# 1444-key attention on one core: score maxima dealt anew over the key tiles, high keys copied a tile sooner

## The reference

```
qm = _split_heads(q @ Wq.T + bq)      # q: layer-normed x, 32 x 100 x 128
km = _split_heads(k @ Wk.T + bk)      # k = v = ctx_1024, 32 x 1444 x 128
vm = _split_heads(v @ Wv.T + bv)
scores = jnp.einsum('bnlh,bnph->bnlp', qm, km) / sqrt(HEAD_DIM)
attn = jax.nn.softmax(jnp.where(mask, scores, MASK_FILL), axis=-1)
out = jnp.einsum('bnlp,bnph->bnlh', attn, vm)
```

## Time and profile before

| | before |
|---|---|
| median of 3 runs | 2171.78 us (2168.76 to 2175.56) |
| the profiled execution, its own time | 2172.06 us |
| its span in the profile | 2170.3 us |
| PE busy | 1935.4 us (89%) |
| DVE busy | 1481.8 us (68%) |
| ACT busy | 1321.2 us (61%) |
| POOL busy | 670.7 us (31%) |
| first `weigh` of the first batch to the last score product | about 603 to 1670 us of the span |

### The profile page before, as it was taken

One profiled execution on the slowest core, in us unless ns is written; L12 is line 12 of the kernel. 1 busy time (PEld: TensorE's weight loads), 2 busy tenths in 40 slices (PEclk: granted clock), 3 DMA queues, 4 the chain that ended last, 5 costly groups with the idle time before them and its releaser, 6 DMA issues. The chain is left out here.

```text
span 2170.3 us, 42902 instructions
## 1 busy us (share of the span) xinstructions
PE 1935.4 (89%) x16792; PEld 1224.2 (56%) x16792; DVE 1481.8 (68%) x3509; ACT 1321.2 (61%) x2169; POOL 670.7 (31%) x605
## 2 busy tenths in 40 slices
PE   3669999766899999999999999999998899999997
PEld 2536766444465656656566565665655455555553
DVE  4844666785778787777877778777783456577541
ACT  2635677586166666666666666666776345666643
POOL 1410223321422131322313223131221323566576
PEclk9879999877599999999999999999999557999998
DMA  5025555001232332323323232232332102221222
GB/s 157 1 69 189 168 186 172 26 27 47 89 106 82 114 119 72 131 82 114 108 84 131 81 115 97 95 131 68 124 105 75 24 12 45 48 41 36 36 70 42
DMA packets 126293, 190.74 MB, mean 88 GB/s; under 512 B 42018, under 2 KB 99466, under 8 KB 125710
## 3 DMA queue, kind: packets, MB, share of 16 engines
q1 hardware_dynamic: 126094, 188.01, 27.9%
HBM read 104.84 MB, written 11.76 MB: 54 GB/s over the span
## 5 line engine op out<-in xcount | busy, mean ns | idle before, releaser
L1607 DVE TENSOR_REDUCE b_part_max<-psum 128x1 f32<-128x482 f32 (+3 forms) x1248 | 738.6, 650 | 200.8 <-PE psum L1493 186.0
L1413 ACT ACTIVATE b_PT<-psum 128x800 f32<-128x800 f32 x768 | 614.9, 836 | 335.4 <-PE psum L1512 329.5
L1493 PE MATMUL psum<-b_KH,b_QBD 64*128 64x482 f32 (+1 forms) x1152 | 416.2, 441 | 37.4 <-DVE b_part_max L1607 35.0
L1512 PE MATMUL psum<-b_QS,b_KS 64*128 64x200 f32 x3072 | 436.7, 288 | 0.3 <-ACT b_PT L1413 0.3
L1512 PEld LDWEIGHTS psum<-b_QS,b_KS 64*128 64x128 f32 x3072 | 346.2, 187 | 15.2 <-issue 10.5
L1528 PE MATMUL psum<-b_PT,b_V 128*32 128x200 f32 x6144 | 341.4, 339 | 0.3 <-ACT b_PT L1413 0.3
L1493 PEld LDWEIGHTS psum<-b_KH,b_QBD 64*128 64x128 f32 x1152 | 194.1, 189 | 182.1 <-DVE b_part_max L1607 115.7
L1338 POOL TENSOR_TENSOR b_KL<-b_KF,b_KH 128x1444 fp32r<-128x1444 f32 x32 | 106.9, 3340 | 589.7 <-PE psum L1512 566.5
L1528 PEld LDWEIGHTS psum<-b_PT,b_V 128*32 128x32 f32 x6144 | 159.9, 109 | 144.6 <-ACT b_PT L1413 78.7
L1814 POOL TENSOR_TENSOR c_HE<-c_HE,c_G 128x400 f32<-128x400 f32 x128 | 131.5, 1032 | 112.6 <-ACT c_HE L1960 106.0
L426 POOL TENSOR_TENSOR a_rs<-a_ve,a_half 100x4 f32<-100x4 f32 x48 | 48.5, 1011 | 312.6 <-DVE a_ve L918 312.5
(11 more groups left out here) (280 smaller groups left out, 2988.2 us busy)
## 6 DMA issues: line engine op xcount, KB each, us to landing
b_KS<-b_KH SPq DMA_DIRECT2D x64, 722.0 KB
a_CT<-in_ctxt SPq DMA_DIRECT2D x32, 722.0 KB, 5.6
b_CT<-in_ctxt SPq DMA_DIRECT2D x32, 722.0 KB, 4.3
b_KS<-b_KL SPq DMA_DIRECT2D x32, 722.0 KB
a_CN<-in_ctxn SPq DMA_DIRECT2D x32, 704.0 KB
c_G<-gates_scratch SPq DMA_DIRECT2D x16, 800.0 KB, 4.3
att_scratch<-b_AO SPq DMA_DIRECT2D x32, 200.0 KB, 5.8
b_MB<-in_mask SPq DMA_DIRECT2D x32, 180.5 KB, 4.4
```

What stands on the lines that cost most here:

```text
L1413: nc.scalar.activation(PT[:, kt % 2, 2 * a:2 * a + 2, :], psum[:, 2 * a:2 * a + 2, 0:TG], ACT.Exp).then_inc(sem["pt_ready"], 1)
L1493: m = mm(bank(b, D, size), QBD[rows, j % 2, tile * D:(tile + 1) * D], KH[rows, j % 2, at_:at_ + size], start=True, stop=True)
L1512: m = mm(bank(p, D, 2 * T, (s % 2) * 2 * T), KS[rows, j % 2, s, kt * D:(kt + 1) * D], QS[rows, j % 2, s * 2 * T:(s + 1) * 2 * T], start=Tr ...
L1607: v.tensor_reduce(part_max[0:rows, q, c:c + 1], bank(b, rows, CHUNKS[c][1]), AX.X, ALU.max)\
```

## The change

Maxima by key tile, in the order of the batch (upper and lower ones added):

| tile | 8 | 9 | 10 | 11 | 0 | 1 | 2 to 6 | 7 |
|---|---|---|---|---|---|---|---|---|
| before | 0 | 4 | 4 | 4 | 4 | 3 | 3 each | 2 |
| after | 2 | 4 | 3 | 3 | 3 | 4 | 3 each | 2 |

`EARLY`, now the count of those in tiles 8 to 11, stays 12. Because tile 8 now has the first maxima of the batch after next, ahead of the "turn" job of the next one, `part_max` gets two buffers; and ACT copies key chunk c behind the exponentials of tile c + 7 instead of c + 8.

```
-MAIN_TILES = ((9, 2, 2), (10, 2, 2), (11, 2, 2), (0, 2, 2), (1, 2, 1), (2, 1, 2), (3, 2, 1), (4, 1, 2), (5, 2, 1), (6, 1, 2), (7, 1, 1))
+MAIN_TILES = ((8, 1, 1), (9, 2, 2), (10, 2, 1), (11, 1, 2), (0, 2, 1), (1, 2, 2), (2, 1, 2), (3, 2, 1), (4, 1, 2), (5, 2, 1), (6, 1, 2),
+              (7, 1, 1))
...
-EARLY = sum(kt > 8 for _, _, _, kt, _ in MAINS)
+EARLY = sum(kt > 7 for _, _, _, kt, _ in MAINS)
...
-        part_max = sb("part_max", [D, QCH, 3])
+        part_max = sb("part_max", [D, 2, QCH, 3])
...
-            pl.memset(part_max[:, :, :], 0.0)
+            pl.memset(part_max[:, :, :, :], 0.0)
...
-                        if kt - 8 in range(len(keys)):
-                            high_keys(place(g, j, keys[kt - 8]), g, j + 2, kt - 8)
+                        if kt - 7 in range(len(keys)):
+                            high_keys(place(g, j, keys[kt - 7]), g, j + 2, kt - 7)
...
-                    v.tensor_reduce(part_max[0:rows, q, c:c + 1], bank(b, rows, CHUNKS[c][1]), AX.X, ALU.max)\
+                    v.tensor_reduce(part_max[0:rows, n % 2, q, c:c + 1], bank(b, rows, CHUNKS[c][1]), AX.X, ALU.max)\
                         .then_inc(drained, 1)
                     if i == MAXES - 1:
                         dve.wait_ge(drained, done)
-                        v.tensor_reduce(mx[:, 0:QCH], part_max[:, :, :], AX.X, ALU.max, negate=True).then_inc(sem["mx_ready"], 1)
+                        v.tensor_reduce(mx[:, 0:QCH], part_max[:, n % 2, :, :], AX.X, ALU.max, negate=True).then_inc(sem["mx_ready"], 1)
```

## The result

The changed kernel takes 2146.81 us (median of 4 runs, 2140.1 to 2149.43), the kernel before, beside it, 2172.74 (4 runs, 2168.76 to 2175.56): a ratio of 0.9875 [0.9849, 0.9901]. I had forecast 2157.2, in a range from 2147 to 2171. The direction was right; the gain, 26 us, is nearly twice the 14.6 of my sum.

What follows compares the result with a forecast made beforehand. VectorE's reductions were taken to pace the four-maxima tiles, the exponentials' floor of 1.89 us the three-maxima tiles. Tile terms summed to -0.485 us a batch, -14.6 over 30 batches, giving 2157.2 us, range 2147 to 2171.

Steps and rivals of the forecast that it cites:

- Tile 8, +0.59: In tile 8, two maxima more: the key waits for the first maximum's bank; 3.05 us for 2.46, +0.59.
- Tiles 9, 10, 11, 0 and 1: Tile 9: 0; 10, 11, 0: -0.55, -0.56, -0.57 us (-0.47 with three queries); tile 1: +0.55 to +0.59.
- High keys a tile sooner, 0: ScalarE's copies of key chunks, ahead of the next tile's exponentials, are hidden by the wait for scores: cost 0.
- The turn later, 0: VectorE starts the turn 0.8 us later, so the maxima's four DMAs issue later, but land in time: cost 0.
- The sum, -14.6: Tile terms of the attention stage: four batches -1.94 us, a batch -0.485, 30 batches -14.6.
- The floor of 1.89: In the last batch, with no jobs, tiles take 1.86 and 1.92 us in turn: the exponentials set a floor of 1.89.
- VectorE's waits for products: A sign to look for: VectorE's waits for products, 186.0 us, should shrink by about what the span does.
- Rival (a): The ring of banks holds three-maxima tiles at 2.06 us, not 1.90: -0.06 a batch, 2170 us; chance 0.17.
- Rival (b): VectorE alone is the bound and tile 8 fills its hole: 1.0 us a batch, 30 us, 2142; chance 0.12.
- Rival (c): The maxima's DMAs land too late, the first score piece waits: +0.28 us a batch, 2180 us; chance 0.09.
- The step that failed: Whole program: -14.6 us against the profiled execution's 2172.06 gives 2157.5; that execution is 0.3 above the median, so 2157.2.

Runs made afterwards that it cites:

- 13 copies: The kernel before with 13 ScalarE copies, one behind the other, as a pause between the attention stage and the last stage: 2169.35 us, 1.0000 [0.9976, 1.0023].
- 7 copies: The changed kernel with 7 ScalarE copies as a pause between the attention stage and the last stage: 2154.38 us, 0.9918 [0.9890, 0.9946] to the kernel before.
- 8 copies: The changed kernel with 8 ScalarE copies as a pause between the attention stage and the last stage: 2149.40 us, 0.9915 [0.9888, 0.9941] to the kernel before.

## Why the prediction was right in its steps and wrong in its size

- **Tile 8, +0.59.** Right: 3.05, by the mechanism named, the key held by the first reduction.
- **Tiles 9, 10, 11, 0 and 1.** Right within 0.02 us, with the one exception of tile 0 with three queries, 3.62 for 3.71: its queries load at 1005.42, 1005.99 and 1006.55, each released by a reduction, 2.06, 2.63 and 3.19 us into the tile. I had put the third at 3.28; the three reductions came 0.57 apart here and not 0.61. That is 0.09 us in 8 batches, 0.7 us in all.
- **High keys a tile sooner, 0.** Right: alone it is worth nothing in either kernel.
- **The turn later, 0.** Right for the reason given: the last of the four DMAs was issued at 998.81, and the first score product that needs them loads its weights at 1002.26 with no DMA among its releasers. When it landed no row shows.
- **The sum, -14.6.** Measured -14.0 in the stage.
- **The floor of 1.89**, put down to the exponentials: the number held (1.88 to 1.92), the reason is not shown. In the earlier trace rows ScalarE is busy for 1.50 of 1.86 and 1.63 of 1.92, TensorE for all of both; each waits for the other in turn.
- **VectorE's waits for products**, to shrink: they grew by 12.7 us, for the reason given above.
- **Rival (a)**, three-maxima tiles at 2.06: refuted, 1.91 and 1.92. **Rival (b)**, VectorE alone: refuted, VectorE still waits 198.7 us for products and the stage gained 14 us, not 30; that the total came near its 2142 is a coincidence. **Rival (c)**: refuted, no wait for a DMA.
- **The step that failed** stands in no sentence of the forecast, only in its arithmetic: "against the profiled execution's 2172.06 that is 2157.5". It holds that everything outside the stage keeps its time, a term of nothing for which no row was read. The last stage did not: 484.8 us for 497.8, with the granted clock at 0.89 for 0.85. I had read a granted clock of 1.00 in every window of the attention stage and not read the windows behind it, where it is at most 0.59 for 129 us. The 0.3 us by which the profiled execution stood above the median of 3 runs said nothing of a program whose runs spread over 26 us; 66 runs have a median 3 us lower.

The 26 us are made up so: 14 from the dealing, shown tile by tile; about 10, an estimate, from less time at the lower clock, which a pause ahead of the last stage can give without the change (13 copies in the kernel before, shown) and perhaps take back (7 copies, indicated only); about 3 of chance in the runs compared. Why the changed kernel spent less time at the lower clock stays open.

## What to carry to other kernels

A stretch with a known pattern can be priced to some hundredths of a microsecond from stretches that already show the pattern: count jobs against banks, and find the drain that each job waits for. A pattern that no stretch shows yet cannot (2.97 us expected, 3.16 measured, for the value between the halves). But where a program passes through a phase of lower clock, its total time is not the old one less the saving: read the granted clock of every stage beside the edited one, give the range its spread, and judge a change of under one per cent by its own stage, or at equal time at the lower clock. To put a job sooner into a ring of banks is worth nothing while its drainer comes as late as before: here it cost 47 us. With the drainer sooner too, the loss was gone, but nothing was gained.

## What was not expected of the hardware

- A pause that puts off the last stage by 9.5 us cost nothing in the kernel before (1.0000 [0.9976, 1.0023]), while the low time fell by 28 us (333 to 305 on the same chip). In the changed kernel 7 copies, which put it off by 4.1 us, go with 11 us more in the mean (2145.8 to 2157.2), and 8 copies with 5 (2150.9); these runs are not all of one chip.
- A microsecond more at the lower level goes with 0.31 us more of the program's time, not with the 0.5 of a program that TensorE alone bounds. The windows above fit that in kind: in the 30 us from 59 us behind the end of the attention stage, TensorE got through 191 instructions at 0.54 and through 229 at 0.89, only 1.2 times as many, for there it was idle for 7.4 us of the 30 and VectorE busy for 21.27.
- Products of 128 rows put between the two halves' work made that work longer: 1.27 us in two parts, and a tile of 3.17 us with PE busy for all of it, where moving the value was expected to save (2.97). The Trainium skill, "TensorEngine Tiling (Array Packing)", section Tiling Modes, Key Properties, says that changing the tiling mode drains TensorE; the value in that place adds such changes, and the trace agrees in sign. That this is the reason was not tested by itself; the halves also run in pairs, and a cut in their work may lose some of that overlap.
- The Trainium skill, "TensorE: Matmul & The Clock Gate", section on the HAM clock gate, What's actually happening, says that the chip judges activity on a count of its own, which does not begin with the kernel. By that rule one and the same kernel would change its clock at other moments from run to run, and the trace agrees in kind: 298 to 371 us of low time in 66 runs of one kernel. It gives no reason why the mean over many runs should change with a pause of fixed length, as it did with 13 copies, and no run here settles that.
